# Layer 1's table copy waits for the first batch of gathered rows

## The reference

```python
h = jnp.maximum(_layernorm(x, axis=-1), 0.0)
x = x + _L0_gnn_ref(h, src, dst, edge_weight, deg_isqrt[:, None], deg_isqrt[:, None])
h = jnp.maximum(_layernorm(x, axis=-1), 0.0)
x = x + _L1_gnn_ref(h, W1, b1, W2, b2, edge_index, 16)

# _L0_gnn_ref: msg = xs[col] * values[:, None]; agg = segment_sum(msg, row)
# _L1_gnn_ref: src, tgt = nn_index
feat = jnp.concatenate([x[tgt], x[src] - x[tgt]], axis=-1)
msg = jax.nn.relu(feat @ W1 + b1) @ W2 + b2
out = segment_sum(msg, tgt) / (deg + 1e-08)
```

## Time and profile before

| | |
|---|---|
| time, median of 3 runs | 2128.58 us (2127.1 to 2130.37) |
| the profiled execution's own time | 2115.95 us |
| its span | 2114.1 us |
| mean granted TensorE clock | 0.914 of full speed |
| PE busy | 1692.6 us, 80% |
| DVE busy | 1465.7 us, 69% |
| POOL busy | 1261.7 us, 60% |
| ACT busy | 1009.9 us, 48% |
| copy queue (q1) | 208.63 MB, 27.4% of 16 DMA engines |
| gathers and scatters (q0) | 128.51 MB, 33.9% |

### The profile page before, as it was taken

The page is one execution under the profiler, slowest core; times in us unless marked ns, Lnnn a source line. Parts: engine busy times, 40 slices in busy tenths (PEclk is TensorE's granted clock), DMA queues, the critical chain, the costliest instruction groups (busy, mean ns, idle before and its releaser), DMA issues.

```text
span 2114.1 us, 45720 instructions
## 1 busy us (share of the span) xinstructions
PE 1692.6 (80%) x13740; PEld 1478.0 (70%) x13740; DVE 1465.7 (69%) x5883; ACT 1009.9 (48%) x2064; POOL 1261.7 (60%) x1004
## 2 busy tenths in 40 slices
PE   4958888887676676620599999999999999999991
PEld 1238877776576566620488889888888888888881
DVE  6969989897677666720477777777767767677660
ACT  0014445443333333310376666767666656666561
POOL 2023323268888878865443433378888888888854
PEclk9979999998888888865799999999999999999996
DMA  7989999856565565545999999955555555555543
GB/s 242 318 295 336 323 334 326 270 103 107 99 109 103 98 105 101 102 50 94 335 326 333 342 336 339 336 114 97 95 94 92 97 94 97 92 97 94 95 65 39
DMA packets 140468, 376.43 MB, mean 178 GB/s; under 512 B 31392, under 2 KB 95657, under 8 KB 127529
## 3 DMA queue, kind: packets, MB, share of 16 engines
q0 software_dynamic: 84672, 128.51, 33.9%
q1 hardware_dynamic: 27452, 208.63, 27.4%
q10 hardware_dynamic: 28304, 38.85, 7.0%
HBM read 323.36 MB, written 258.12 MB: 275 GB/s over the span
## 4 chain that ended last, share of the span: by engine, by line
POOL 21%; PE 18%; issue 11%; DMA 3%; ACT 0%; DVE 0%; ACTq 0%; POOLq 0%; DVEq 0%
POOL table_out L937 11%; POOL ends L925 10%; PE ps_h L1249 10%; PE ps_m L1263 5%; DMA table_out<-e_ring,e_targets_all 2%; PE ps_t L1236 2%; PE ps_s L1276 2%; ACT ends L1148 0%; DMA ends<-x,keys 0%; DVE e_moments L999 0%; ACT hid L1162 0%; DVE out_sum L1071 0%; ACTq L1133 0%; POOLq L935 0%; DVE out_lo L1076 0%
## 5 line engine op out<-in xcount | busy, mean ns | idle before, releaser
L925 POOL DMA_INDIRECT ends<-x,keys x392 | 399.3, 1019 | 306.9 <-PE ps_h L1249 109.0
L774 PE MATMUL ps_deg<-table,hot 128*128 128x128 bf16 x5488 | 352.9, 226 | 80.4 <-issue 72.6
L774 PEld LDWEIGHTS ps_deg<-table,hot 128*128 128x128 bf16 x5488 | 328.7, 101 | 99.7 <-issue 91.0
L467 POOL DMA_INDIRECT x<-sums_ring,targets_all x196 | 323.4, 1650 | 89.0 <-issue 63.5
L937 POOL DMA_INDIRECT table_out<-e_ring,e_targets_all x196 | 319.9, 1632 | 92.2 <-issue 55.9
L457 POOL DMA_INDIRECT rows<-in_x,row_idx x196 | 205.1, 1046 | 240.9 <-ACT normed L702 188.3
L1249 PE MATMUL ps_h<-feat_hi,w_hi 128*128 128x512 f32 x784 | 314.2, 401 | 9.4 <-DVE feat_lo L1066 4.8
L1249 PE MATMUL ps_h<-feat_lo,w_hi 128*128 128x512 f32 x784 | 310.4, 396 | 0.0
L1249 PE MATMUL ps_h<-feat_hi,w_lo 128*128 128x512 f32 x784 | 310.3, 396 | 0.0
L788 PE MATMUL ps_sum<-msg_hi,same 128*128 128x260 f32 x784 | 151.0, 322 | 137.7 <-issue 131.2
L1263 PE MATMUL ps_m<-w_hi,hid_hi 128*128 128x256 f32 x784 | 227.9, 291 | 9.8 <-DVE hid_lo L1061 8.3
(11 more groups left out here) (141 smaller groups left out, 3447.2 us busy)
## 6 DMA issues: line engine op xcount, KB each, us to landing
table_out<-x SPq DMA_DIRECT2D x400, 252.0 KB
x<-in_x SPq DMA_DIRECT2D x400, 250.0 KB
hi_row<-hi_rows ACTq DMA_DIRECT2D x49, 256.0 KB
src_row<-src_rows ACTq DMA_DIRECT2D x49, 256.0 KB
dst_row<-dst_rows ACTq DMA_DIRECT2D x49, 256.0 KB
ends<-x,keys POOLq DMA_INDIRECT x392
rows<-in_x,row_idx POOLq DMA_INDIRECT x196
x<-sums_ring,targets_all POOLq DMA_INDIRECT x196
```

The source lines that it names most:

```text
L467: pool.indirect_dma_start(out=x1_d, out_offset=bass.IndirectOffsetOnAxis(ap=targets_all[:, b, j:j + 1], axis=0), in_=sums_ring[:, b % RING ...
L774: last = nc.tensor.matmul(ps_deg[q][k][:, j * P:(j + 1) * P], hot[:, c, k, j * P:(j + 1) * P], table[:, c, part, :], start=(c == 0 and par ...
L925: pool.indirect_dma_start(out=ends[b % NE][:, n, :], out_offset=None, in_=x1_d, in_offset=bass.IndirectOffsetOnAxis(ap=keys[:, 1 - end, at ...
```

## The change

In layer 1 SP now waits until the eight gathers of batch 0 have landed before it issues the first piece of the copy. The same semaphore at the same value already holds back POOL's gathers of batch 1. Nothing else differs.

```diff
             @block.sync
             def _(sp):
+
+                sp.wait_ge(ends_in[0], 16 * 2 * W)
                 for k in range(FLIGHT):
                     sp.dma_start(out_flat[k], x1_flat[k]).then_inc(bulk_out[k], 16)
                 with sp.Fori(1, ROUNDS) as r:
```

## The result

The changed kernel takes 2136.61 us (median of 18 runs, 2131.92 to 2139.77) beside 2127.84 us of the kernel before (18 runs, 2123.44 to 2136.51). The ratio is 1.0043, with a 95% interval of 1.0034 to 1.0052: **9.2 us slower** (7.2 to 11.1). The forecast was slower by 4.9 us, 2133.5 us, in a range of 2128.5 to 2140.5. The sign and the change of gate were right, the forecast size was about half of the measured one.

A forecast was written before the change was run, and what follows sets the result against it. PE's pacing of the gathers before layer 1's first scatter was taken as the bound; copy delay 12.7 less relief 2.0 and slack 5.9, plus 0.1 to wake POOL, gave +4.9 us: 2133.5 us, range 2128.5 to 2140.5.

The forecast's parts named there:

- The gate before is the pacing, the gate after is the copy: Layer 1's first scatter: held by gathers paced to PE until 1385.2 before, by the copy's end at 1390.0 after.
- SP starts 12.7 us later: Start of layer 1's copy: SP's first issue moves from 994.51 to batch 0's landing at 1007.2.
- the price of the earlier trace: Batch 0's gathers in layer 1: 2.80 us from issue to landing, read from a scatter-phase gather; forecast took 2.9.
- PE 4.5 us earlier: Start of layer 1: PE's first real matmuls come 6.4 to 1.4 us earlier, taken as 4.5, through earlier landings.
- Everything behind the first scatter is rigid: Layer 1 from first scatter to span end: POOL's chain stays 728.9 us long and moves as a whole.
- The first scatter 4.9 us later: POOL in layer 1: first scatter at 1390.1 instead of 1385.2, with 0.1 us to wake POOL after the copy.
- The forecast's own sign for that: Layer 1's first scatter: a start after 1393 would make the delay's relief or the landing wrong.
- The slack of 5.9 us: Layer 1 before the change: copy ends at 1379.3, 5.9 us ahead of the first scatter at 1385.2.
- The relief of 2.0 us: Layer 1's copy: net 0.5 MB of other traffic leaves its saturated stretch, so it ends 2.0 us sooner.
- the brisk first 9 us: Start of layer 1's copy: 406 GB/s assumed again; at 336 the copy ends at 1391.9 instead of 1390.0.
- The rival that the slack isn't there: Layer 1's copy already the gate in timed runs, 1.5% or more slower: +10.7 us, 2139.3; chance 0.21.
- The 12.6 us between the profiled execution and the timed runs: Whole kernel: profiled execution 2115.95 against timed median 2128.58, a difference of 12.6 us carried over to the forecast.

The follow-up runs named there:

- e1: Changed kernel with SP waiting for ACT's first key load instead of batch 0's gathers; ratio 0.9998 against the kernel before, -0.4 us.
- e2: Changed kernel with SP waiting until batches 0 and 1 have both landed; ratio 1.0083 against the kernel before, +17.7 us.
- f1: Kernel before with the scatter phase's gathers spread wider, 13/5 instead of 11/4 per group of two scatters; ratio 1.0020 against the kernel before.
- f3: Changed kernel with the scatter phase's gathers spread 13/5 instead of 11/4 per group of two scatters; ratio 1.0032 against the kernel before.

## Why the prediction came out as it did

- **The gate before is the pacing, the gate after is the copy.** Right: a gap of 0.30 us became 18.02 us, and e1 and e2 name the copy as what ended it.
- **SP starts 12.7 us later.** 12.55 us (12.40 and -0.15 from ACT's first issue). Batch 0's eighth gather was issued at 1012.97 and had landed by 1015.76, 2.8 us; the price of the earlier trace rows held.
- **PE 4.5 us earlier.** 5.8 us in the first pair of profiles (32.2 against 38.0), 5.0 in the second pair (33.5, 38.5), 6.6 between f1 and f3 on the third chip (41.9, 35.2). Batch 1's landing beside the fresh copy took 5.0 us from its last issue (1024.77 to 1029.75), between the 4.3 and 9.3 of the forecast. As forecast it was worth nothing.
- **Everything behind the first scatter is rigid.** Right for this change: 728.9 and 728.6 us. f1 shows how near its end is: 26 us of later gathers suffice to hand the end over to PE.
- **The first scatter 4.9 us later.** This is the sum that was off: 12.3 us in the first pair of profiles, 9.2 in the timed runs. Two terms stood between the 12.7 us of SP and the 4.9, and both were too large. The forecast's own sign for that was a first scatter after 1393; counted from where the stage began in the first profile it came at 994.66 + 402.84 = 1397.5.
  - *The slack of 5.9 us.* I took the copy's end to be the moment at which the data rate drops, 1379.3. The copy's last packet ended at 1380.33, and a scatter that waits for it starts 1.3 us behind that, where I had allowed 0.1. With both the slack in the profile was 3.5 us, and in four more executions of the same code 0.7 to 5.6, in the mean 3.6.
  - *The relief of 2.0 us.* The reckoning in megabytes is sound as a sum, but the copy shows nothing of it: to its last packet it took 388.4 us without the wait and 388.8 with it, in the mean of six and four profiles. With a spread of 4 us among the six the difference of the means is uncertain by 1.7 us, which leaves room for 1.2 us of relief at most. The bytes did leave, even 0.8 MB where I had 0.5. But the brisk first 9 us, which the forecast assumed to come again, did not: 351 GB/s instead of 406, 0.5 MB less, which is 1.5 us at 336 GB/s, of the 1.9 that the forecast had named for this case. That this is what ate the relief fits in size and was not tested by itself.
  - *Put together.* SP's 12.55 us, less the mean slack of 3.6 and with no relief, make 9.0, and the timed runs have 9.2 (7.2 to 11.1). In the first pair it is 12.55 + 3.3 - 3.5 = 12.3, where 3.3 us are the copy's own length (389.1 against 385.8): the first profile had the shortest copy of all six without the wait. e1 fits as well: a delay of 3.6 us, all of it slack, costs nothing that can be told.
- **The rival that the slack isn't there** gave 10.7 us, nearer to the 9.2 than the forecast, but partly by luck: it left out a slack of which 3.6 us exist and kept a relief of 2.0 us that doesn't show, and the two errors partly cancel. Its reason, a copy 1.5% slower in the timed runs, holds in part at most: to the last packet the copy was 385.8 us in the profile that I read and 387.5 to 390.2 in the five others, 0.4 to 1.1% more, while the pacing ended later, too.
- **The 12.6 us between the profiled execution and the timed runs** were carried over whole, and that was right for the total. 7.5 us of them had come about before layer 0's first scatter (438.42 against 445.90), none in the scatter chain of layer 1 (728.9 against 729.0). But 1 to 4 us arise in layer 1 ahead of the first scatter (390.5 against 391.8 to 394.2), where copy and pacing run side by side, and that is where the slack is made.

## What to carry to other kernels

When a change delays a transfer that another engine waits for, date its end by the last packet of its own queue plus the way to the instruction that it releases, taken from a place where it is the gate, and not by the last slice with much traffic: here the two differ by 2.4 us of the 5.9 that I counted on. A slack of a few microseconds read from one profiled execution needs a second and a third execution, if possible on another chip, before a forecast is built on it: here they gave 3.5, 0.7 and 3.9. And where two chains run side by side, a head start for the one is worth something only after the other has its own gate covered: the same wait cost 9.2 us with 20 batches gathered ahead and gained 4 to 5 with 21.

## What was not expected of the hardware

- A first scatter that waits for the copy starts 1.29 to 1.36 us behind the last packet of the copy's queue in six profiles of seven, 1.66 in the seventh.
- The copy of 103 MB took 379.8 to 390.4 us from the first to the last issue in the fourteen profiled executions, and 384.2 to 393.7 to its last packet, though it is the same copy beside nearly the same gathers. In three executions of one kernel it was 381.4, 382.6 and 386.3 to the last issue. To the last packet profiles on one chip lie closer: 387.5, 388.2 and 388.4 on the third without the wait.
- Two gathers in a group of two scatters are all but free to the chain (6.5 us for a group, 6.4 without gathers), and a third costs 1.3 us: eight gathers fewer shortened the chain by 3 to 4 us instead of 10.2.
- A copy that starts when the first eight gathers have landed had 341 to 351 GB/s over all queues in the 9 us from 3.5 us after its first issue on, one that starts together with them 363 to 406.
- With half a batch of gathers rushed in beside the end of the copy, the copy was 390.4 and 387.4 us long, above the twelve other executions (at most 386.3). The cause wasn't found.
